# Residual built on chip, shorter quantiser chains, and a block-by-block last projection in a fused two-layer encoder

## The reference

```python
    h = _L0_tok_ref(x, L0_tok_W, L0_tok_b)                     # patches @ W + b
    h = jnp.concatenate([h, _L0_txt_ref(x_txt, L0_txt_emb)], axis=1)
    h = h + _L0_attn_ref(_layernorm(h), ...)    # LayerNorm again, two Mamba-2 scans, MLP with two GELUs, LayerNorm
    h = h + _L0_ffn_ref(_layernorm(h), ...)     # fake-quantised MLP, below
    h = h + _L1_attn_ref(_layernorm(h), ...)    # 12 heads of 64
    h = h + _L1_ffn_ref(_layernorm(h), ...)     # shared expert + 8 routed experts, top 2
```

```python
        xq = fq_act_asym(x_smoothed)    # min and max of all of x: scale, zero point, round, clip to 0..255
        h = jnp.einsum('bnc,hc->bnh', xq, fq_weight(w1_smoothed)) + b1
        h = jax.nn.gelu(h, approximate=False)
        hq = fq_act_sym(h)              # max |h|
        out = jnp.einsum('bnh,ch->bnc', hq, fq_weight(w2)) + b2
        out = fq_act_asym(out)          # min and max of all of out
```

## Time and profile before

| | us |
|---|---|
| Median of 3 runs | 780.86 (779.29 to 783.02) |
| Profiled execution: whole run | 782.75 |
| Profiled execution: span from first to last instruction | 780.9 |
| TensorE busy, products | 647.4 (83%) |
| VectorE busy | 488.0 (62%) |
| ScalarE busy | 367.5 (47%) |
| GpSimd busy | 276.9 (35%) |
| Mean granted TensorE clock, share of full | 0.894 |

### The profile page before, as it was taken

One profiled execution on the slowest core, in us unless ns is written; L12 is line 12 of the kernel. 1 busy time (PEld: TensorE's weight loads), 2 busy tenths in 40 slices (PEclk: granted clock), 3 DMA queues, 4 the chain that ended last, 5 costly groups with the idle time before them and its releaser, 6 DMA issues.

```text
span 780.9 us, 13384 instructions
## 1 busy us (share of the span) xinstructions
PE 647.4 (83%) x4906; PEld 579.6 (74%) x4906; DVE 488.0 (62%) x1262; ACT 367.5 (47%) x846; POOL 276.9 (35%) x293
## 2 busy tenths in 40 slices
PE   2239898898899726448899999799989999999994
PEld 2229776578898612227788888698989999999994
DVE  2277779662331787681787785468538777877851
ACT  0027876861343436434656644342126655655541
POOL 3633515433020325002333232301131766756633
PEclk9758999995999956657999999879979999999998
DMA  7810000223000190200000002102064676787843
GB/s 219 184 43 4 2 1 1 92 85 98 1 1 1 53 225 0 91 21 4 2 4 7 4 5 83 45 1 112 10 244 136 177 245 200 218 248 201 213 128 67
DMA packets 30412, 67.89 MB, mean 87 GB/s; under 512 B 6890, under 2 KB 20755, under 8 KB 28011
## 3 DMA queue, kind: packets, MB, share of 16 engines
q0 software_dynamic: 13200, 48.20, 21.2%
q1 hardware_dynamic: 17147, 18.84, 8.8%
HBM read 60.90 MB, written 6.61 MB: 86 GB/s over the span
## 4 chain that ended last, share of the span: by engine, by line
PE 60%; DVE 12%; ACT 4%; issue 3%; POOL 2%; another core or an unknown queue 1%; POOLq 0%; DVEq 0%; ACTq 0%
PE bank L1812 10%; PE bank L1772 4%; PE bank L1776 4%; PE bank L1775 4%; PE bank L1774 4%; PE bank L1773 3%; PE bank L1695 2%; PE bank L1631 2%; PE bank L1674 2%; PE bank L1344 1%; PE bank L1485 1%; PE bank L1509 1%; PE bank L1510 1%; PE bank L1511 1%; PE bank L1403 1%
## 5 line engine op out<-in xcount | busy, mean ns | idle before, releaser
L2403 DVE TENSOR_SCALAR big<-bank 128x256 f32<-128x256 f32 (+1 forms) x126 | 52.1, 414 | 60.1 <-PE bank L1776 54.6
L1240 ACT ACTIVATE big<-bank 128x256 f32<-128x256 f32 (+1 forms) x126 | 47.7, 379 | 57.1 <-PE bank L1776 53.5
L796 POOL TENSOR_TENSOR big<-big,arc 128x423 f32<-128x423 f32 (+1 forms) x48 | 37.8, 816 | 77.4 <-DVE arc L2348 77.4
L823 POOL DMA_INDIRECT total<-big,goal x32 | 53.5, 1673 | 23.8 <-issue 17.3
L1772 PE MATMUL bank<-x_lead,w_lead 128*128 128x256 f32 x192 | 56.5, 294 | 0.1
L1775 PE MATMUL bank<-x_both,w_lead 128*128 128x256 f32 x192 | 54.5, 284 | 0.0
L1776 PE MATMUL bank<-x_both,w_rest 128*128 128x256 f32 x192 | 54.1, 282 | 0.0
L1774 PE MATMUL bank<-x_lead,w_rest 128*128 128x256 f32 x192 | 54.0, 281 | 0.0
L1773 PE MATMUL bank<-x_rest,w_lead 128*128 128x256 f32 x192 | 53.9, 281 | 0.0
L830 POOL DMA_INDIRECT big<-x_rows,origin x32 | 32.9, 1029 | 49.5 <-DVE goal L2460 23.1
L2414 DVE SCALAR_TENSOR_TENSOR big<-big 128x256 f32<-128x256 f32 (+1 forms) x126 | 50.2, 409 | 0.1
(11 more groups left out here) (530 smaller groups left out, 2014.8 us busy)
## 6 DMA issues: line engine op xcount, KB each, us to landing
big<-in_patches SPq DMA_DIRECT2D x1, 1536.0 KB, 7.6
areg<-in_e_gate_up SPq DMA_DIRECT2D x1, 1536.0 KB, 6.4
shared_lead<-in_e_gate_up POOLq DMA_DIRECT2D x1, 1536.0 KB, 6.9
wreg<-in_ffn_w SPq DMA_DIRECT2D x1, 1152.0 KB
ffw_lead<-in_ffn_w POOLq DMA_DIRECT2D x1, 1152.0 KB, 6.0
out<-total SPq DMA_DIRECT2D x2, 423.0 KB
wreg<-in_in_w SPq DMA_DIRECT2D x2, 419.0 KB
wreg<-in_in_w SPq DMA_DIRECT2D x4, 209.5 KB
```

What stands on the lines that cost most here:

```text
L823: pool.indirect_dma_start(out=total, in_=YS[:, j % 2, q * D:(q + 1) * D], in_offset=None, out_offset=bass.IndirectOffsetOnAxis(ap=goal[:, ...
L1240: nc.scalar.activation(GS[:, n % 3, 0:w], bank[2 * (n % 2)][:, 0:w], ACT.Silu).then_inc(S["g_silu"], 1)
L2403: v.tensor_scalar(UM[:, n % 3, 0:w], bank[2 * (n % 2) + 1][:, 0:w], 10.0, -10.0, ALU.min, ALU.max).then_inc(S["u_clip"], 1)
```

## The change

Five places change.

1. *Start.* The trip through DRAM is gone. Two shift matrices (ones on a shifted diagonal, made by GpSimd) let TensorE place the image rows (`place`) and the ids of the words (`parts`) at the rows of the tiles; GpSimd gathers nine times 128 embedding rows straight into tile order, and VectorE adds both (`together`). Everything up to the normalised tokens goes in three groups. `shf` and the patches are issued from ScalarE's queue. The rounded weights are loaded ahead of the gather. `first_tokens` makes ScalarE write four results per group instead of two; `project(0)` stands ahead of the transposes of group 2.
2. `tokens_out(0)` comes after tile 5 instead of 6.
3. *Quantiser.* The three GpSimd reductions become `spread` on TensorE (a column repeated as weights, times the identity: each partition gets the whole column) and a maximum on VectorE. `asym` is split into `step_size` and `limits`. Weight scaling is shared with ScalarE, in two halves.
4. *Output and third LayerNorm.* The output's range is read from PSUM; the transposes come before the rounding; rounding, addition and LayerNorm go by pairs and groups; GpSimd normalises group 0. The values of the last rows move behind the first scores.
5. *End.* The last `down` goes block by block, and the second half of the output is copied from ScalarE's queue.

The core of the diff (buffers, names and the repeated uses of banks are left out):

```diff
             load(gatew[0:DB, 1, :], i["gate_w"][DA:D, :], "ld_small")
             load(gateb[:, :], i["gate_b"].partition_broadcast(P).rearrange("p a n -> p (a n)"), "ld_small")
 
-            sp.wait_ge(S["img_ready"], 2)
-            for b in range(NB):
-                sp.dma_start(h0[b, 0:NI, :], img[(b % 2) * NI:(b % 2 + 1) * NI, b // 2, :]).then_inc(S["h_loaded"], 16)
-            sp.wait_ge(S["txt_ready"], 3)
-            sp.dma_start(h0[:, NI:L, :].rearrange("b n d -> n b d"), txt).then_inc(S["h_loaded"], 16)
-            sp.wait_ge(S["h_loaded"], 16 * (NB + 1))
-            hf = h0.rearrange("b n d -> (b n) d")
-            sp.wait_ge(S["padded"], 1)
-            sp.dma_start(H[:, 0:TT - 1, :], hf[0:(TT - 1) * P, :].rearrange("(t p) d -> p t d", p=P)).then_inc(S["h_loaded"], 16)
-            sp.dma_start(H[0:LAST, TT - 1, :], hf[(TT - 1) * P:T, :]).then_inc(S["h_loaded"], 16)
-
             sp.wait_ge(S["dt_act"], 8)
             for d in range(2):
...
-            for k in range(2):
-                at = slice(k * T // 2, (k + 1) * T // 2)
-                sp.dma_start(of[at, :], total[at, :]).then_inc(S["total_in"], 16)
+            sp.dma_start(of[0:T // 2, :], total[0:T // 2, :]).then_inc(S["total_in"], 16)
             sp.wait_ge(S["total_in"], 64)
...
+
+            pool.wait_ge(S["txt_ready"], 3)
+            for t in range(TT):
+                pool.indirect_dma_start(out=words[:, t, :], out_offset=None, in_=i["emb"],
+                                        in_offset=bass.IndirectOffsetOnAxis(ap=ids[:, t:t + 1], axis=0))\
+                    .then_inc(gathered[t // 3], 16)
...
             pool.wait_ge(S["hq_mm"], 1)
+            pool.tensor_tensor(QKL[:, :], qk_full[:, :], QKH[:, :], ALU.subtract).then_inc(S["att_rest"], 1)
...
+            pool.wait_ge(S["rstd_ready"], 4)
+            for t in range(3):
+                pool.tensor_scalar(X[:, t, :], H[:, t, :], mv[:, t, 0:1], rstd[:, t:t + 1], ALU.subtract, ALU.mult).then_inc(ln_x, 1)
```

```diff
+            def first_tokens(g):
+
+                act.wait_ge(ln_turned, g + 1)
...
+                wa, wb = ln1[:, 0, :], ln1[0:DB, 1, :]
+                cols = slice(g * CM, (g + 1) * CM)
+                nc.scalar.activation(XS1[g % 2][:, 0, :], a[:, 0:CM], ACT.Identity, scale=wa[:, 0:1], bias=wa[:, 1:2])
+                nc.scalar.activation(XAH[:, cols], a[:, 0:CM], ACT.Identity, scale=wa[:, 0:1], bias=wa[:, 1:2]).then_inc(ln_out, 1)
...
+            deviations(0, ln_var, 3, ln_std)
+            second_deviations(0)
+            deviations(1, ln_var, 6, ln_std)
+            second_deviations(1)
+            deviations(2, ln_var, 9, ln_std)
             act.wait_ge(S["ld_inw"], 16 * 8)
-            ln(0, ln1)
+            first_tokens(0)
+            second_deviations(2)
+            first_tokens(1)
+            first_tokens(2)
 
             for k in range(8):
...
                     deviations(t // 3, S["ln2_var"], t + 1, S["ln2_std"])
+                    if t == 5:
+                        tokens_out(0)
                     if t == TT - 1:
                         tokens_out(1)
                     deviations(t // 3, ln_var, TT + t + 1, ln_std)
...
+            def scaled(n):
+
+                t, u = OT_PAIRS[n]
+                r = rows(u - 1)
+                act.wait_ge(S["oq_turned"], n + 1)
+                nc.scalar.activation(Y[0:r, t:u, :], bank[OT_BANK[n]][0:r, 0:(u - t) * D].rearrange("p (t d) -> p t d", d=D), ACT.Identity,
+                                     scale=qs[0:r, 46:47], bias=cst[0:r, 1:2]).then_inc(S["om_ready"], 1)
...
+            scaled(3)
+            whole(2)
+            deviations(0, ln_var, 2 * TT + 3, ln_std)
+            scaled(4)
```

```diff
+            for n, (t, b, row) in enumerate(parts):
+                at = P - (b * L + NI - t * P)
+                last = mm(bank[4][:, 2 * t:2 * t + 2], shift[0:NX, at:at + P], pick[:, b, :],
+                          start=n == 0 or parts[n - 1][0] != t, stop=n + 1 == len(parts) or parts[n + 1][0] != t)
+            last.then_inc(S["scoreT"], 1)
+
+            def place(j):
+
+                pe.wait_ge(S["img_ready"], j + 1)
+                for b in (2 * j, 2 * j + 1):
+                    for t, a, z in IMG_ROWS[b]:
+                        s_, at = (shift_odd, P + NI) if b % 2 else (shift_even, P)
+                        at -= b * L - t * P
+                        owners = [c for c in range(NB) for u, _a, _z in IMG_ROWS[c] if u == t]
+                        k, o = IMG_AT[t]
...
-            pe.wait_ge(S["in_lead"], 16 * 6)
-            pe.wait_ge(S["in_rest"], 4)
+                last.then_inc(S["img_mm"], 1)
+                if j == 1:
+                    pe.wait_ge(S["txt_ready"], 3)
...
+            def spread(o, col, n):
+
+                for k in range(n):
+                    last = mm(o[:, k * P:(k + 1) * P], qs[:, col + k:col + k + 1].to_broadcast([P, P]), ident, start=True, stop=True)
+                last.then_inc(S["ranges_all"], 1)
...
-                    pe.wait_ge(S["ot_ready"], 6)
-                o = bank[4 + t % 4]
-                nc.tensor.transpose(o[0:rows(t), 0:DA], OT[:, 0, t * P:t * P + rows(t)], ident)
-                nc.tensor.transpose(o[0:rows(t), DA:D], OT[0:DB, 1, t * P:t * P + rows(t)], identw[0:DB, 0:DB]).then_inc(S["oq_turned"], 1)
-
-
-            turn(2, X)
-            pe.wait_ge(ln_out, LN_BASE[3])
-            pe.wait_ge(S["xa_rest"], 12)
+            for n, (a, z) in enumerate(OT_PAIRS):
+                for t in range(a, z):
+                    pe.wait_ge(S["ot_ready"], 2 * ((t * P + rows(t) - 1) // CH + 1))
+                    o, at = bank[OT_BANK[n]], (t - a) * D
+                    nc.tensor.transpose(o[0:rows(t), at:at + DA], OT[:, 0, t * P:t * P + rows(t)], ident)
+                    last = nc.tensor.transpose(o[0:rows(t), at + DA:at + D], OT[0:DB, 1, t * P:t * P + rows(t)], identw[0:DB, 0:DB])
+                last.then_inc(S["oq_turned"], 1)
+            pe.wait_ge(S["or_ready"], 1)
+            spread(bank[3], 40, 2)
+
+
+            turn(2, X, (0, 1))
...
+            turn(2, X, (2,))
+            query_key(0, range(3, 12))
+            pe.wait_ge(S["xa_rest"], 12)
+            scores(0, 0)
             pe.wait_ge(S["att_rest"], 7)
-            values([0, 1], NB * R, [x[:, :] for x in TAILS])
...
+                    for k in range(KH):
+                        pe.wait_ge(S["hh_ready"], KH * g + k + 1)
+                        for q in range(GCH):
+                            at = k * SLOTS + q * P
+                            last = mm(result(g, q), HH[:, g % 2, at:at + P], W[:, W2 + k * D:W2 + (k + 1) * D],
+                                      start=k == 0, stop=k == KH - 1)
+                            if k == KH - 1:
+                                last.then_inc(S["e_mm"], 1)
+                    return
                 for q in range(TOK(kind, c) // P):
                     for k in range(KH):
```

```diff
+            def together(g):
+
+                dve.wait_ge(gathered[g], 48)
+                dve.wait_ge(S["img_mm"], IMG_PLACED[g + 1])
+                if g == 2:
+                    dve.wait_ge(S["padded"], 1)
+                for t in range(3 * g, 3 * (g + 1)):
+                    k, at = IMG_AT[t]
+                    r = rows(t)
+                    st.add(v.scalar_tensor_tensor(out=H[0:r, t, :], in0=words[0:r, t, :], scalar=known[0:r, t:t + 1], in1=bank[k][0:r, at:at + D],
+                                                  op0=ALU.mult, op1=ALU.add))
+                st.wait()
+                for t in range(3 * g, 3 * (g + 1)):
+                    st.add(v.bn_stats(stats[:, t, :], H[:, t, :]))
...
+            def step_size(src, scale, inv):
+
                 st.add(v.tensor_tensor(qs[:, scale:scale + 1], qs[:, src:src + 1], qs[:, src + 1:src + 2], ALU.add))
                 st.wait()
                 st.add(v.tensor_scalar(qs[:, scale:scale + 1], qs[:, scale:scale + 1], 1.0 / 255, QEPS, ALU.mult, ALU.max))
                 st.wait()
-                st.add(v.reciprocal(qs[:, inv:inv + 1], qs[:, scale:scale + 1]))
-                st.wait()
...
+            def limits(src, inv, lo, hi):
+
+                st.add(v.tensor_scalar(qs[:, lo:lo + 1], qs[:, src + 1:src + 2], qs[:, inv:inv + 1], ROUNDER, ALU.mult, ALU.add))
+                st.wait()
+                st.add(v.tensor_scalar(qs[:, lo:lo + 1], qs[:, lo:lo + 1], -1.0, 2 * ROUNDER, ALU.mult, ALU.add))
                 st.wait()
                 st.add(v.tensor_scalar(qs[:, hi:hi + 1], qs[:, lo:lo + 1], 255.0, None, ALU.add))
                 st.wait()
-
...
             st.add(v.tensor_reduce(qs[:, 50:56], qw1, AX.X, ALU.max, apply_absolute_value=True))
             st.wait()
             st.add(v.tensor_scalar(qs[:, 50:56], qs[:, 50:56], 1.0 / 127, QEPS, ALU.mult, ALU.max))
             st.wait()
-            st.add(v.reciprocal(qs[:, 56:62], qs[:, 50:56]))
-            st.wait()
-            for k in range(KH):
```

(20 more changed lines are left out.)

386 lines of the change are left out of this document (233 added, 153 removed).

## The result

The changed kernel takes 778.32 us (median of 20 runs, 775.78 to 780.13) beside 781.62 us for the kernel before on the same chip: ratio 0.9953, 95% interval 0.9938 to 0.9968. The forecast was 751.0, range 743 to 761. The profiled execution after has a span of 776.7 us and took 778.4, against 780.9 and 782.75 before; the granted clock is 0.917 on average.

The account below looks back on a forecast made before the run. It saw a serial start with nothing dense until 58.82 us, then LayerNorm and quantiser chains of waiting engines. Gains of 30.6 from 782.75 gave 752.2, less 1.9 for the median 750.3, stated as 751; range 743 to 761.

Parts of the forecast that it names:

- part 1: Start: on-chip placing and gathers replace the DRAM trip, third group enters the projection near 40 instead of 58.82; 18.5 us gained.
- The gathers land after 31: Sign at the start that would show the forecast wrong; gathered words were expected landed by 28.7.
- Late gathers: Rival at the start: gathered words land only after the rounded-weight loads drain, near 35; gain 12, total 757; 14%.
- The stretch from the first projection to the second LayerNorm changes by more than 1 us: Sign that would show the forecast wrong: this stretch, with no instruction edited, was expected to keep its length.
- rigid shift: Expected wherever no instruction is edited, as from first projection to second LayerNorm: everything moves in time, lengths unchanged.
- The residual is not on the path: Rival at the start: another condition holds the old place, so the start gives 0 to 2; total 769; 3%.
- Part 2: Second LayerNorm: ScalarE's first token copy moves ahead of table loads and activations, ending VectorE's wait; 1.7 us gained.
- part 3: Quantiser's first range: reduction moves from GpSimd to TensorE, weight scaling shared with ScalarE; 0.5 us gained.
- part 4: Quantiser's second range: a TensorE matmul and VectorE maximum, 1.1, replace GpSimd's reduction, 6.0; 4.9 us gained.
- Part 5: Output range, rounding, third LayerNorm: scaling 2.2 later, scores 6.8 earlier, 2.0 given back at the tails' values; 4.8 gained.
- part 6: The end: 0.4 lost by block-by-block last products, 0.6 gained by output issues side by side; net 0.2 gained.
- The clock: Rival at 59 to 142 us: 2.4 GHz reached only late after the thinner start, possibly 795 in all; 3%.

Follow-up runs that it names:

- next_first: Changed kernel with the third token window loaded before the image embedding's weights instead of behind them: 0.9808 of the kernel before.
- scalar_prod: Changed kernel, third window and token bias loaded earlier, output range spread earlier, variance-times-reciprocal product with one tile operand: 0.9729 of the kernel before.
- lead_later: As scalar_prod, but GpSimd issues the projection's rounded-weight loads only after VectorE's match: 0.9740 of the kernel before.
- range_pool: Changed kernel, third window and token bias loaded earlier, second range reduced by GpSimd again: 5.84 us from maximum to scalar chain; run once, only trace places read.
- after_again: The changed kernel word for word, rerun on another chip: 0.9942 of the kernel before.
- best: Changed kernel, third window and token bias earlier, two weight subtractions and third LayerNorm's first normalisation on VectorE, output range spread earlier: 0.9809 of the kernel before.

## Why the prediction was wrong

**The step that failed** is in part 1: "one of the two loads that the match needs goes out on ScalarE's queue and the third is not waited for". The third is waited for, by the picks, which stand on the way to the indices (L1990 waits on ld_next), and the change had put it behind 576 KB on SyncE's queue with 1536 KB beside it on ScalarE's. The diff showed all of this: a wait had been moved from one instruction to a later one of the same chain and was taken for removed. In the forecast this wait stands at nothing; next_first gives its price: 11.95 at the picks, 12.0 at the third group.

The other 17 of part 1's 29 us:
- The match at 10.43, not 5.8: 4.6. I carried over the 3.4 from the last issue to the landing, and it did not hold for earlier issues; without the patches beside the windows the match came at 8.36 at best, about where it was before (8.53). Why is open.
- Placing takes 5.71 instead of 2.1, 3.6 more: the 13 small matmuls are 26 records of 0.22, and I priced them like eight transposes (1.29).
- "I expect 27 and the gather to be last": in the changed kernel the first three tiles wait for the image products (47.36 <-PE), since VectorE's order has three image additions ahead of them. From there each group takes 4.0, the first 6.1 with the 3.03 of L2030; the third starts 10.1 behind the first. I had the first two groups done while the gathers still ran. From the first gather to the third group's residual it takes 22.9 (34.54 to 57.48) where 13.2 were forecast (15.5 to 28.7), 9.7 more, the largest of the three. Only behind that did the working hold: 11.8 from the third group's residual to its projection, 11.4 forecast.

With all of it repaired as far as I got (scalar_prod, lead_later), the third group enters at 54.5, 4.3 ahead of the kernel before; no version came nearer to 18.5.

The forecast named its own signs. *The gathers land after 31* came: the first is issued at 34.54. But the rival *Late gathers* was not the reason; no wait of the changed kernel ends with words. *The stretch from the first projection to the second LayerNorm changes by more than 1 us* came by the letter too: from the first group's entry it grew by 2.3 (55.04 to 260.27, 63.11 to 270.62), because the third group follows the first by 6.2 instead of 3.8. From the third group's entry on it kept its length to 0.1, and that was meant by a rigid shift. The rival nearest in time, *The residual is not on the path* (769), had the wrong mechanism: the residual is on the path, and it comes later.

**What held.** Part 2 (-1.8 for -1.7), part 3 (-0.8 for -0.5) and part 4 (-4.9 for -4.9), whose mechanism range_pool shows. Part 5: -4.2 for -4.8, by its own steps: scaling later by 3.3 (340.41 - 334.21 - 2.9) for 2.2, scores 2.75 earlier than before or 5.65 by the part alone, for 6.8, and 1.45 given back at the tails' values for 2.0. Of the 1.1 by which scaling came later than that, 0.7 is there at ScalarE's last copy of the output (it ends at 335.02, for 331.4 + 2.9): ScalarE's copies now wait for VectorE's reading of the same bank (0.25 each), which the working left out. Part 6 had the sign wrong: 0.2 lost up to the scatter, and 0.4 behind the output's issue (0.2 in after_again) where 0.6 was to be gained; each is a few tenths. Its sign, a first scatter 3.9 after the last up product, could not have come, since it is 4.97 in the kernel before and part 6 expected to lose: 3.9 is the time to the end of the first half's products, and ScalarE's scaling and the handover to GpSimd follow.

**What no part had.** 3.6 us between the attention loop and the last product. Most of them stand at the gate, where the edits change nothing: its 36 matmuls take 7.9 before and 5.3 after. The first 18 of them, before and then after:

```profile
506.09 4.01 PE L1741 MATMUL bank<-gatew,XTa 128*128 128x8 f32 x18 [0.94 <-ACT XTb L901]
```

```profile
504.46 2.17 PE L1837 MATMUL bank<-gatew,XTa 128*128 128x8 f32 x18 [0.94 <-ACT XTb L902]
```

The granted clock is 0.50 from 506 to 514 before, the level of 1.2 GHz, and 0.78 from 504 to 510 after, where the first 18 ran at 2.4. This is no accident of one execution of the changed kernel: the first 18 take 2.2 to 2.4 in sixteen of the seventeen traces of changed versions (4.01 in best); all 36 take 6.1 in after_again. Of the kernel before there is one trace, so whether it always meets the half clock there is not shown. Without this and the smaller steps behind it the two spans would differ by 0.6 us, so that this gain, which no part forecast, is luck. *The clock* was a rival with 3%, for a loss of a whole stage; as a shift of a few us it decides between two versions of this kernel.

## What to carry to other kernels

When a wait moves from one instruction to another of the same chain, find the load it is for and price its place in the queue; "not waited for here" is not "not waited for". When a serial start is replaced by several short steps, name for each group what gates it and let the groups queue on the engine they share, since the last group's time is the sum. An instruction that is made earlier can land in another engine's busy time and return the gain: look at what stands in the window it moves into.
